# Attention with a null key: the sums' banks drained by two additions in place of three, and eight low halves of a head pair on VectorE

## What is computed

```python
q = l2norm(q) * q_scale
k = l2norm(k) * k_scale
sim = einsum('bhid,bjd->bhij', q, k) * 8.0 + attn_bias      # with the null key in front
sim = where(causal, neg, sim); sim = where(mask, sim, neg)
attn = softmax(sim, axis=-1)
out = einsum('bhij,bjd->bhid', attn, v)
x = x + ffn(ln(out @ Wout, g_out))
```

## Time and profile before

| | us |
|---|---|
| median of 3 runs | 1657.63 |
| lowest, highest | 1653.59, 1662.75 |
| profiled execution, its time | 1657.8 |
| profiled execution, span | 1656.0 |

### The profile page before, as it was taken

One profiled execution on the slowest core, in us unless ns is written; L12 is line 12 of the kernel. 1 busy time (PEld: TensorE's weight loads), 2 busy tenths in 40 slices (PEclk: granted clock), 3 DMA queues, 4 the chain that ended last, 5 costly groups with the idle time before them and its releaser, 6 DMA issues.

```text
span 1656.0 us, 39721 instructions
## 1 busy us (share of the span) xinstructions
PE 1508.3 (91%) x13844; PEld 987.3 (60%) x13844; DVE 1325.0 (80%) x2295; ACT 1076.6 (65%) x2168; POOL 1333.7 (81%) x924
## 2 busy tenths in 40 slices
PE   4988985999999999997998985999999999999797
PEld 2444443777777777775444442777777777777342
DVE  4456995798888888885898995888888888888597
ACT  4665664778778788787112664787787787787210
POOL 4664665999999999998564764999999999999563
PEclk9999996999999999999999997999999999999899
DMA  6004764111111111111796775112112012010596
GB/s 201 1 7 87 141 136 81 40 27 40 39 27 40 35 32 40 30 23 27 147 190 147 147 141 108 40 33 47 26 28 52 21 32 52 15 38 2 118 185 156
DMA packets 225620, 114.93 MB, mean 69 GB/s; under 512 B 193200, under 2 KB 193712, under 8 KB 225456
## 3 DMA queue, kind: packets, MB, share of 16 engines
q1 hardware_dynamic: 220864, 104.42, 30.6%
q10 hardware_dynamic: 4608, 8.39, 1.4%
HBM read 58.11 MB, written 8.54 MB: 40 GB/s over the span
## 4 chain that ended last, share of the span: by engine, by line
PE 53%; DVE 12%; issue 12%; DMA 6%; POOL 5%; ACT 2%; SPq 2%; DVEq 1%; ACTq 0%; POOLq 0%
PE ps L1300 23%; PE ps L1273 11%; PE ps L1276 10%; DVE work L1039 5%; PE ps L1339 5%; PE ps L1242 3%; DMA qo<-work 2%; DVE work L1067 2%; DMA work<-work 2%; SPq L445 1%; POOL work L589 1%; DMA tab<-bias_table 1%; POOL tab L566 1%; PE ps L1348 1%; DVE quot L996 1%
## 5 line engine op out<-in xcount | busy, mean ns | idle before, releaser
L576 POOL TENSOR_TENSOR work<-work 128x1024 f16<-128x1024 f32 (+2 forms) x576 | 978.1, 1730 | 54.6 <-ACT work L740 51.8
L1039 DVE SCALAR_TENSOR_TENSOR work<-ps,tab 128x1024 f32<-128x1024 f32 (+3 forms) x640 | 669.2, 1060 | 168.1 <-PE ps L1276 148.3
L740 ACT ACTIVATE work<-work 128x1024 f32<-128x1024 f32 (+3 forms) x640 | 578.1, 924 | 225.0 <-DVE work L1039 220.2
L1300 PEld LDWEIGHTS ps<-vals,work 128*128 128x128 bf16 (+1 forms) x8704 | 545.3, 98 | 115.8 <-POOL work L576 2.4
L1300 PE MATMUL ps<-vals,work 128*128 128x129 f16 x8704 | 600.6, 221 | 1.9 <-POOL work L576 1.8
L1273 PE MATMUL ps<-qo,kT 128*128 128x512 f16 (+3 forms) x1280 | 346.4, 353 | 36.7 <-DVE work L1039 21.8
L1276 PE MATMUL ps<-qo,kT 128*128 128x512 f16 (+3 forms) x1280 | 344.5, 351 | 0.0
L1276 PEld LDWEIGHTS ps<-qo,kT 128*128 128x128 f16 x1280 | 123.7, 99 | 119.2 <-issue 6.1
L1339 PE MATMUL ps<-wout,work 128*128 128x512 f16 x768 | 175.9, 388 | 15.6 <-DMA work<-work 15.6
L1242 PE MATMUL ps<-wq,tab 128*128 128x512 f16 x768 | 180.0, 385 | 9.7 <-DMA tab<-tab 9.5
L1339 PEld LDWEIGHTS ps<-wout,work 128*128 128x128 f16 x768 | 76.4, 100 | 110.3 <-DMA work<-work 16.0
(11 more groups left out here) (132 smaller groups left out, 1323.3 us busy)
## 6 DMA issues: line engine op xcount, KB each, us to landing
tab<-bias_table SPq DMA_DIRECT2D x64, 512.0 KB, 4.7
tab<-in_x SPq DMA_DIRECT2D x64, 256.0 KB, 3.1
out_x<-work ACTq DMA_DIRECT2D x32, 256.0 KB, 3.0
work<-in_L_cond_Wq SPq DMA_DIRECT2D x1, 2048.0 KB, 10.0
work<-in_L_cond_Wout SPq DMA_DIRECT2D x2, 1024.0 KB, 10.0
qo<-in_L_cond_w SPq DMA_DIRECT2D x1, 1024.0 KB, 7.3
work<-work SPq DMA_TRANSPOSE x64, 4.3
qo<-in_L_cond_b SPq DMA_DIRECT2D x2, 256.0 KB, 5.5
```

The lines of the kernel that those rows point to most:

```text
L576: pool.tensor_tensor(low[:, k % LRING, :, c0:512], probs[:, r, :, c0:512], high[:, r, :, c0:512], ALU.subtract).then_inc(low_pool, 1)
L740: act.activation(probs[:, k % RING, :, c0:512], probs[:, k % RING, :, c0:512], ACT.Exp).then_inc(expd, 1)
L1039: dve.scalar_tensor_tensor(out=probs[:, k % RING, :, c0:512], in0=ps[:, 2 * (k % 2):2 * (k % 2) + 2, c0:512], scalar=SCORE, in1=tab[:, :, ...
L1300: last = pe.matmul(ps[:, sum_bank(i, q), (t % SUMS) * VS:(t % SUMS + 1) * VS], parts[:, rings[part], e, s * P:(s + 1) * P], vals[:, j, :], ...
```

## The change

Three things, all on VectorE's side of the attention:

- The columns of `vals` change places: high part, ones, low part. The first addition of a drain then takes the high sums and the denominators together (65 columns a tile) plus the null key's 65 into `o_part`, the second adds the low sums into `o_sum`. The addition into `denom` is gone. The reciprocal reads the denominators from `o_part` and comes after the second addition.
- `o_part` holds all eight tiles, and so is shared by the drains of a block; the waits ahead of a drain are for the last block's reciprocal and for the additions one block back. ScalarE's store waits for the block's own reciprocal under a count that is one higher.
- `DVE_LOW` has eight units in place of four. GpSimd's list is the rest, 32 in place of 36. The score products stay as they were.

```diff
-DVE_LOW = (7, 11, 22, 27)
+DVE_LOW = (6, 9, 11, 16, 18, 22, 24, 29)
...
-        o_part = carve(work, SUMS, DH)
+        o_part = carve(work, 8, VW)
...
-                    act.wait_ge(o_rec, m + 1)
+                    act.wait_ge(o_rec, m + 2)
...
-                        dve.tensor_scalar(vals[:, :, 2 * DH:VS].rearrange("p t o -> p (t o)"),
+                        dve.tensor_scalar(vals[:, :, DH:VW].rearrange("p t o -> p (t o)"),
...
-                    dve.scalar_tensor_tensor(out=vals[:, t, DH:2 * DH], in0=v,
+                    dve.scalar_tensor_tensor(out=vals[:, t, VW:VS], in0=v,
...
-                    dve.tensor_tensor(denom[:, i % 2, t0:t0 + n], acc[:, :, 2 * DH],
-                                      null_tmp[:, i % 2, t0:t0 + n, DH], ALU.add).then_inc(o_den, 1)
-                    dve.wait_ge(o_added, 3 * m + q + 6)
-                    dve.tensor_tensor(o_part[:, 0:n, :], acc[:, :, DH:2 * DH],
-                                      null_tmp[:, i % 2, t0:t0 + n, 0:DH], ALU.add).then_inc(o_low, 1)
+                    part = o_part[:, t0:t0 + n, :]
+                    dve.wait_ge(o_rec, m + 1)
+                    dve.wait_ge(o_added, 3 * m + q + 4)
+                    dve.tensor_tensor(part, acc[:, :, 0:VW], null_tmp[:, i % 2, t0:t0 + n, :], ALU.add).then_inc(o_part_in, 1)
+                    dve.wait_ge(o_part_in, 3 * m + q + 1)
+                    dve.tensor_tensor(o_sum[:, i % 2, t0:t0 + n, :], acc[:, :, VW:VS], part[:, :, 0:DH], ALU.add
+                                      ).then_inc(o_added, 1)
                     if q == 2:
-                        dve.wait_ge(o_den, 3 * m + 3)
-                        dve.reciprocal(rec[:, i % 2, :], denom[:, i % 2, :]).then_inc(o_rec, 1)
-                    dve.wait_ge(o_low, 3 * m + q + 1)
-                    dve.tensor_tensor(o_sum[:, i % 2, t0:t0 + n, :], acc[:, :, 0:DH], o_part[:, 0:n, :],
-                                      ALU.add).then_inc(o_added, 1)
+                        dve.reciprocal(rec[:, i % 2, :], o_part[:, :, DH]).then_inc(o_rec, 1)
```

More of the change, by code:

```diff
@@ L68 @@
 LRING = 8
-WORK = 16912
+WORK = 16928
 OUT_AT = 4096
@@ L233, in build @@
         rinv = sb("rinv", [P, 2, H + 1], F32)
-        denom = sb("denom", [P, 2, 8], F32)
         rec = sb("rec", [P, 2, 8], F32)
@@ L326, in build @@
             "b_qn", "b_kn", "b_hi", "b_khi", "b_lo", "b_klo", "b_turned", "b_cd", "b_snd", "b_pn"))
-        tab_ld, scored, biased, expd, pv_done, summed, null_ready, o_low, o_added, o_den, o_rec, o_stored = (
-            sem(n) for n in ("tab_ld", "scored", "biased", "expd", "pv_done", "summed", "null_ready", "o_low",
-                             "o_added", "o_den", "o_rec", "o_stored"))
+        tab_ld, scored, biased, expd, pv_done, summed, null_ready, o_part_in, o_added, o_rec, o_stored = (
+            sem(n) for n in ("tab_ld", "scored", "biased", "expd", "pv_done", "summed", "null_ready", "o_part_in",
+                             "o_added", "o_rec", "o_stored"))
         low_dve, low_pool, b_vh, b_vl = (sem(n) for n in ("low_dve", "low_pool", "b_vh", "b_vl"))
@@ L809, in _ @@
             for s, n in ((b_xn, 2), (b_qn, 2), (b_ss, 1),
-                         (b_vl, 1), (b_snd, 2), (b_rinv, 2), (biased, CB), (o_added, 6), (c_y1, 2), (c_fin, 2),
+                         (b_vl, 1), (b_snd, 2), (b_rinv, 2), (biased, CB), (o_added, 6), (o_rec, 1), (c_y1, 2), (c_fin, 2),
                          (c_zn, 2), (c_as, 2), (c_yq, 1)):
```

## The result

The changed kernel takes 1801.97 us (median of four runs, 1795.43 to 1802.15), the kernel before beside it 1660.1 us: 1.0851 times as long, interval 1.0808 to 1.0894. It is slower by 8.5%; predicted were 1794 us, 1738 to 1828. The profiled execution took 1802.03 us, with a span of 1800.2 us and a mean granted clock of 0.947.

The account below looks back on a forecast made before the run. TensorE was taken to set the pace, with VectorE breaking it for at most 2.8 us a pair. 1657.8 us plus 100 for late bias additions over 16 pairs plus 36 for half clock gave 1794 us, range 1738 to 1828.

Parts of the forecast that it names:

- The ledger: Start times worked out through slots 18 to 23 and 31 to 34: score 23 late by 4.09 us, score 34 by 2.34.
- The low half: On VectorE in attention, meeting GpSimd in mid-operation: 1.46 us wait plus 1.22, 2.68 us; next bias addition 1.83 late.
- VectorE comes first: Rival: GpSimd starts later, VectorE finds the way free; 2.29 us a pair, 37 in all, 1694 us; chance 0.10.
- The three low halves charged at nothing: Units 6, 9 and 24 (slots 8, 11, 26), no drain right behind: 0 us, bounds 0 and 0.3 each.
- the jams: Late bias additions in slots 18 to 23 and 31 to 34: with drains' -0.18, 6.25 us a pair, 100 in all.
- The drain of 0.66 us: VectorE's drain of three tiles falls from 0.73 to 0.66 us; six on the path give -0.18 us a pair.
- The clock: TensorE's idle pieces in attention bring half-clock stretches: 21 of 32, each costing 1.7 us, 36 us; bounds 0 and 54.
- Two of three: Share of idle pieces followed by half clock, from three TensorE waits in the projections; gave 21 of 32.
- No loss of clock: Rival: same lateness in attention, but TensorE's idle pieces don't lower the clock; 1758 us, chance 0.23.
- GpSimd sets the pace: Rival: GpSimd's fullness holds TensorE back; taking its units returns up to 2.8 us a pair, 45 us, 1613; chance 0.06.
- Worse: Rival: every idle piece lowers the clock (54 us) and three cheap low halves cost 0.3 each (14); 1826 us, chance 0.08.

Follow-up runs that it names:

- the idle filled: Changed kernel plus 32 unused matmuls of 125 columns behind the sum products of slots 22 and 33: 1753.91 us, ratio 1.0614.
- three ahead: Changed kernel with low halves 16, 18 and 29 run before their slot's bias addition in place of after it: 1674.57 us, ratio 1.0131.
- five low halves without the jams: Changed kernel without units 16, 18 and 29 in VectorE's list, leaving 6, 9, 11, 22 and 24: 1647.25 us, ratio 0.9968.
- The drains alone: Changed kernel with the old list of low halves on VectorE (7, 11, 22, 27): 1649.85 us, ratio 0.9981.
- without 29: Changed kernel with unit 29 back on GpSimd: 1735.89 us, ratio 1.0491.
- without 16 and 18: Changed kernel with units 16 and 18 back on GpSimd: 1688.12 us, ratio 1.0213.
- one operand: Changed kernel with VectorE's eight low halves reading one SBUF operand (high half times a constant), so not the true low halves: 1742.29 us, ratio 1.0547.
- the list alone: Kernel before, with its old drains, given the new list of eight low halves on VectorE: 1796.79 us, ratio 1.0873.
- the drains dealt out: Changed kernel with most drains one or three slots later and four low halves on VectorE (9, 12, 24, 33): 1632.93 us, ratio 0.9877.

## Why the prediction was right

**The ledger** holds to a few hundredths, but for one idle time. All times from the start of bias 18 (515.16) and of bias 31 (541.87):

| step | predicted | measured |
|---|---|---|
| bias 19 | 3.60 | 3.59 |
| bias 20 | 5.40 | 5.38 |
| low half in slot 20 reached | 6.54 | 6.51 |
| bias 21 | 9.63 | 9.60 |
| score 23 | 10.85 | 10.87 |
| bias 32 | 4.26 | 4.26 |
| score 34 | 5.48 | 5.53 |
| TensorE idle ahead of score 23, score 34 | 2.46, 2.63 | 2.28, 2.68 |

The idle time ahead of score 23 is 0.18 us shorter, as slot 22 ends 1.94 us after its score product starts, in place of 1.77. The pair follows from the ledger: 62.70 + 6.25 = 68.95 us was predicted at the full clock, and the kernel with the idle filled, at the full clock, has 68.94 (late by 4.11 and 2.39, less the 0.25 of the drains).

**The low half** was put at 2.68 us and took 2.53. The prediction added 1.22 to the wait of 1.46, but by its own row the operation ends 1.08 us after GpSimd's, which gives 2.54. The ledger counted with the 1.08, and so the next instruction starts at 3.59 after the bias addition, where 3.60 was predicted. (The operation of 17 columns and 1.77 us is a multiplication, not an addition; its own line takes 0.18 at its shortest, so the argument stands.)

**Who arrives first** decided, as the rival "VectorE comes first" said it would: 1.22 us and 1.31% when it does (three ahead), 2.5 us and 8.51% when it doesn't. GpSimd's start 0.43 us ahead of VectorE was predicted, 0.44 to 0.46 measured.

**The three low halves charged at nothing**, and the drains: five low halves without the jams give a pair of 62.22 us, so 0 was right. The drain of 0.66 us is exact (519.88 to 520.54). The drains alone give back 3.5 us (the medians), where -0.18 a pair were counted on the path, or 2.9 us.

**The clock** is the term that was mis-sized, twice over, in opposite directions: 21 stretches of 1.7 us each were predicted (36 us), and 30 came, behind 32 spells, at 1.1 to 1.65 us each, 45 us in all. From the late score product on, slots 23 and 24 take 5.21 us in place of 3.56 at the full clock, in all 16 pairs, and slots 34 and 35 take 3.79 to 4.12 in place of 2.67, in 14. A stretch costs less than 1.7 where TensorE also stands in it: in the one from 403.20 it works for 3.00 of 3.40 us. The filled idle gives the same 45 us. The forecast had the count too low and the price too high, so it is partly luck that 36 came as near. "Two of three" was read off three spells in another stage, and could not carry more.

**The sum.** 100 for the jams and 36 for the clock were predicted. Measured: (68.94 - 62.75) x 16 = 99 us and 45 us, 144 us together. The two profiled executions differ by as much (1802.03 less 1657.8); the medians differ by 141.9 us, and the interval of the ratio is some 7 us to either side.

**The rivals.** "No loss of clock" falls with the half-clock stretches and the filled idle. "GpSimd sets the pace" falls with GpSimd's 18.4 us of idle time a pair and no gain from its four units fewer. "Worse" named 32 stretches; 30 came, at a lower price.

**Still open:** which idle spells lower the clock. 2.28 us did in all 16 pairs (without 29; once it was 2.45), 2.68 us did in none of 16 (without 16 and 18), and 2.14 us did in 5 of 16 (one operand). Two spells a pair did in 30 of 32 (the changed kernel, 2.28 and 2.68) and in 25 of 32 (the list alone, 2.28 and 2.74). The length of the spell doesn't decide alone; what else does, these runs don't show, and none of them varies what stands ahead of a spell by itself.

## What to carry to other kernels

Room on an engine is room only where its partner isn't in mid-operation: look at which engine arrives first at each meeting, since the later one pays the rest of the other's operation. A delay costs nothing in a slot with slack behind it and everything in a slot with a drain behind it, so write the times of start into a ledger until the next thing that TensorE waits for; summed busy time tells neither. Before moving work to the freer engine, move what makes its full slots full: with the drains dealt out, and four low halves kept away from them, the kernel gained 1.2% where the move lost 8.5%.

## What the runs showed of the hardware

**A wait between VectorE and GpSimd is for the whole operation, and depends on the form.** Behind GpSimd's 1.89 us: two inputs from SBUF, 1.22 us alone and 2.53 in the meeting; one input from SBUF in a quick form, 0.68 alone and 2.00 in the meeting; one input from SBUF and one from PSUM, 1.22 in both. With VectorE first it is GpSimd that stretches, from 1.89 to 2.29 and 2.37. The Trainium skill, "SBUF — State Buffer", section "SBUF: two separate sides", says that VectorE in a two-port mode, or with two inputs from SBUF, and GpSimd share one pair of ports, that the first to start holds it for its whole operation, and that the other is blocked. The three forms agree with that. My own wording had left out the quick one; that it ran in a two-port mode fits its 0.68 us and its wait, but no run here shows the mode itself.

**Idle spells of TensorE of 2.14 to 2.74 us can be followed by half the clock**, 1.2 GHz for 3.4 us, in mid-attention: 30 of 32 at 2.28 or 2.68 us in the changed kernel, 5 of 16 at 2.14 us with one operand. The Trainium skill, "TensorE: Matmul & The Clock Gate", section "Why this matters for your kernels", warns only of longer idle times; these rows go against it as a safe bound, and the run without 16 and 18, with no loss behind 2.68 us, shows that such a spell is no sure loss either.

**Added matmuls can shorten a kernel.** 64 matmuls a pair whose output nothing reads took the ratio from 1.0851 to 1.0614.
